# The routing's row one-hots as sixteen 16-bit comparisons with a column scalar, in a block with two mixtures of experts around attention

## The reference

```python
x = x + 0.5 * _L0_ffn_ref(_layernorm(x), router_weight, w_in, w_out, bias)
x = x + _L0_attn_ref(_layernorm(x), w_q, w_k, w_v, w_o, b_o)
x = x + 0.5 * _L0_ffn_ref(_layernorm(x), router_weight, w_in, w_out, bias)
```

## Time and profile before

| what | us |
|---|---|
| median of 3 runs (lowest, highest) | 451.69 (450.56, 455.47) |
| profiled execution, from the first to the last instruction | 448.6 |
| what lies around that span: the median less the span | 3.1 |
| TensorE busy | 401.3 (89%) |
| VectorE busy | 302.4 (67%) |
| ScalarE busy | 257.7 (57%) |
| GpSimd busy | 269.0 (60%) |
| the row one-hots (L945), four operations in all | 6.8 |
| w_lo on VectorE (L892), eight operations | 13.4 |
| TensorE's mean granted clock, as a share of full speed | 0.954 |

### The profile page before, as it was taken

How to read it: one execution, slowest core, us unless ns; L and a number is a source line. 1 busy time by engine, 2 the same in 40 slices (tenths; PEclk the granted TensorE clock), 3 DMA queues, 4 the chain that set the end, 5 groups by cost and what they waited for, 6 DMA issues and landing times.

```text
span 448.6 us, 10288 instructions
## 1 busy us (share of the span) xinstructions
PE 401.3 (89%) x2892; PEld 330.1 (74%) x2893; DVE 302.4 (67%) x605; ACT 257.7 (57%) x630; POOL 269.0 (60%) x314
## 2 busy tenths in 40 slices
PE   7305999999999989889999999988899999999995
PEld 3302788888888876758788888766478888888884
DVE  6795855685565688697767677775556576655656
ACT  2561656555655645688778788832065565565552
POOL 5846874686547817857757777410255576755760
PEclk9555899999999999999999999998899999999999
DMA  8748841111212180000000000004571112211136
GB/s 276 287 187 300 282 136 58 47 57 37 70 49 49 43 273 8 1 1 3 4 0 0 0 0 0 1 1 153 162 249 53 54 35 70 59 58 47 47 85 222
DMA packets 25736, 38.87 MB, mean 87 GB/s; under 512 B 3056, under 2 KB 20720, under 8 KB 25712
## 3 DMA queue, kind: packets, MB, share of 16 engines
q1 hardware_dynamic: 19088, 24.41, 16.1%
q0 software_dynamic: 4544, 12.07, 8.9%
q10 hardware_dynamic: 2080, 2.10, 1.4%
HBM read 29.37 MB, written 9.19 MB: 86 GB/s over the span
## 4 chain that ended last, share of the span: by engine, by line
PE 65%; DVE 16%; DMA 7%; POOL 3%; ACT 3%; issue 3%; SPq 0%; DVEq 0%; ACTq 0%; POOLq 0%
PE bank L1326 24%; PE bank L1348 12%; PE bank L1483 7%; PE bank L1494 4%; PE bank L1336 4%; DMA arena<-xn_scratch,gather_row 3%; PE bank L1450 2%; PE bank L1302 2%; PE bank L1249 2%; DMA w_out<-y_scratch 2%; PE bank L1530 2%; DVE w_lo L892 2%; POOL w_lo L511 2%; DMA y_scratch<-arena,scatter_row 1%; PE bank L1484 1%
## 5 line engine op out<-in xcount | busy, mean ns | idle before, releaser
L524 POOL DMA_INDIRECT arena<-xn_scratch,gather_row x46 | 52.8, 1149 | 58.1 <-PE bank L1302 35.6
L530 POOL DMA_INDIRECT y_scratch<-arena,scatter_row x42 | 59.3, 1412 | 31.6 <-ACT arena L701 28.6
L1326 PE MATMUL bank<-w_hi,xT_hi 128*128 x184 | 62.4, 420 | 2.1 <-ACT xT_hi L664 2.1
L1018 DVE TENSOR_TENSOR wo_lo<-w_out,wo_hi 128x1024 fp32r<-128x1024 f32 x46 | 62.0, 1348 | 2.9 <-PE bank L1348 2.0
L1023 DVE TENSOR_TENSOR gT_lo<-bank,gT_hi 128x512 fp32r<-128x512 f32 x46 | 31.7, 690 | 45.4 <-ACT gT_hi L679 45.4
L1326 PE MATMUL bank<-w_lo,xT_hi 128*128 x184 | 58.0, 396 | 0.0
L1326 PE MATMUL bank<-w_hi,xT_lo 128*128 x184 | 57.8, 395 | 0.0
L617 POOL TENSOR_TENSOR k_head<-k_hi,head_mask 128x256 fp32r<-128x256 f32 x64 | 38.8, 627 | 28.8 <-PE bank L1484 21.7
L690 ACT ACTIVATE wo_hi<-w_out 128x1024 fp32r x46 | 48.8, 1061 | 9.5 <-issue 8.7
L672 ACT ACTIVATE arena<-bank 128x512 f32<-128x512 f32 x46 | 27.5, 598 | 42.9 <-PE bank L1326 42.9
L1007 DVE TENSOR_TENSOR xT_lo<-bank,xT_hi 128x256 fp32r<-128x256 f32 x46 | 19.5, 424 | 43.0 <-ACT xT_hi L664 43.0
(11 more groups left out here) (180 smaller groups left out, 979.9 us busy)
## 6 DMA issues: line engine op xcount, KB each, us to landing
w_out<-in_win_t SPq DMA_DIRECT2D x8, 1024.0 KB, 5.1
w_out<-in_wout_t SPq DMA_DIRECT2D x16, 512.0 KB, 6.0
w_out<-y_scratch SPq DMA_DIRECT2D x16, 256.0 KB, 4.4
xn_scratch<-arena ACTq DMA_DIRECT2D x2, 1024.0 KB, 6.1
x<-in_x SPq DMA_DIRECT2D x4, 256.0 KB, 3.7
out<-x SPq DMA_DIRECT2D x4, 256.0 KB, 2.2
arena<-xn_scratch,gather_row POOLq DMA_INDIRECT x46, 3.4
y_scratch<-arena,scatter_row POOLq DMA_INDIRECT x46, 3.0
```

The costliest lines, as they stand in the source:

```text
L524: pool.indirect_dma_start(out=xb[j % 2][:, :], out_offset=None, in_=xn_dram, in_offset=bass.IndirectOffsetOnAxis(ap=gather_row[:, j:j + 1] ...
L530: pool.indirect_dma_start(out=y_dram, in_=y[j % 2][:, :], in_offset=None, out_offset=bass.IndirectOffsetOnAxis(ap=scatter_row[:, j:j + 1], ...
L1018: dve.tensor_tensor(wo_lo[:, :, :], w_out[:, bass.ds(e, 1), :, :].rearrange("p o c d -> p (o c) d"), wo_hi[u][:, :, :].bitcast(F32), ALU.s ...
L1326: last = pe.matmul(bank[2 * half + u][:, :], tok[u][:, k, :], wts[:, bass.ds(e, 1), k, half * H:(half + 1) * H], start=(part == 0 and k == ...
```

## The change

Two operations of 128 x 1024 elements, each comparing a 32-bit integer array with a 32-bit float array, become sixteen of 128 x 128, each comparing the 16-bit `col_h` with one column of the 16-bit `row_h` as a scalar per partition. The operation changes its kind from one with two array operands (tensor_tensor) to one with an array and a scalar (tensor_scalar). GpSimd makes col_h once at the start, one more constant; VectorE makes row_h from row_i in each routing. The first eight comparisons move behind the first form of block_of, the other eight behind `past`. The idle products of TensorE in the second routing go from 18 to 13.

```diff
--- before.py
+++ after.py
@@ -52,7 +52,7 @@
 LOOPED = (BLOCKS - 2 - PEELED) // 2
 AFTER = PEELED + 2 * LOOPED
 STAGES = 3
-CONSTS = 20
+CONSTS = 21
 IDENT_CONSTS = 3
 KSLOTS = 2
 P_SCALE = 2.0 ** 15
@@ -66,7 +66,7 @@
 POOL_LEAD = 1
 BIAS_STEP = 4
 
-WARM_START, WARM_RANKS, WARM_PLAN, WARM_TURNED = 12, (0, 18), (8, 6), (0, 4)
+WARM_START, WARM_RANKS, WARM_PLAN, WARM_TURNED = 12, (0, 13), (8, 6), (0, 4)
 WARM_END, WARM_CONTEXT, WARM_SCORES, WARM_LAST = 2, 4, 7, 3
 WARM_TURN = (5, 3)
 TPAIRS = TILES // 2
@@ -192,6 +192,8 @@
         before = sb("before", [P, P], F16)
         ones = sb("ones", [P, P], F16)
         col = sb("col", [P, P])
+        col_h = sb("col_h", [P, P], F16)
+        row_h = sb("row_h", [P, PAIRS], F16)
         block_edge = sb("block_edge", [P, E])
         expert_before = sb("expert_before", [P, E, E])
         block_no = sb("block_no", [P, BLOCKS])
@@ -492,6 +494,7 @@
             iota(block_no[:, :], [[1, BLOCKS]], 0, 0)
             inverse_root(0, 1)
             iota(col[:, :], [[1, P]], 0, 0)
+            then(pool.tensor_copy(col_h[:, :], col[:, :]))
             inverse_root(0, 2)
             iota(tile_edge[:, :], [[P, TILES]], 0, 0)
             inverse_root(0, 3)
@@ -940,16 +943,15 @@
                 dve.wait_ge(route_step, over_at)
                 first_at = mark(dve.tensor_reduce(first_block[:, :], over_edge[:, :, :], AX_X, ALU.add))
 
-                def one_hot_rows(q):
-                    shape = [P, q.stop - q.start, P]
-                    return mark(dve.tensor_tensor(row_hot[:, q, :], bc(row_i[:, q], 2, shape), bc(col[:, :], 1, shape),
-                                                  ALU.is_equal))
+                def one_hot_rows(some):
+                    for q in some:
+                        dve.tensor_scalar(row_hot[:, q, :], col_h[:, :], row_h[:, q:q + 1], None, ALU.is_equal)
 
 
                 dve.wait_ge(route_step, row_at)
                 if f == 0:
                     split_low(2)
-                one_hot_rows(slice(0, PAIRS // 2))
+                row_at = mark(dve.tensor_copy(row_h[:, :], row_i[:, :]))
                 dve.wait_ge(route_step, first_at)
                 placed_at = mark(dve.tensor_tensor(placed[:, :, :, :], choice[:, :, :, :],
                                                    first_block[:, :].unsqueeze(1).unsqueeze(1).to_broadcast(both), ALU.mult))
@@ -957,7 +959,8 @@
                 dve.wait_ge(route_step, placed_at)
                 block_at = mark(dve.tensor_reduce(block_of[:, :].rearrange("p (k i) -> p k i", k=TOPK), placed[:, :, :, :],
                                                   AX_X, ALU.add))
-                one_hot_rows(slice(PAIRS // 2, PAIRS))
+                dve.wait_ge(route_step, row_at)
+                one_hot_rows(range(0, PAIRS // 2))
                 if f == 0:
                     split_low(3)
                 dve.wait_ge(route_step, block_at)
@@ -966,6 +969,7 @@
                 past_at = mark(dve.tensor_tensor(past[:, :, :], bc(end_block[:, :], 1, [P, BLOCKS, E]),
                                                  bc(block_no[:, :], 2, [P, BLOCKS, E]), ALU.is_le))
                 dve.wait_ge(route_step, block_at)
+                one_hot_rows(range(PAIRS // 2, PAIRS))
                 then(dve.tensor_tensor(blk_hot[:, :, :], bc(block_of[:, :], 2, [P, PAIRS, BLOCKS]),
                                        bc(block_no[:, :], 1, [P, PAIRS, BLOCKS]), ALU.is_equal))
                 dve.tensor_tensor(blk_pair[:, :, :], blk_hot[:, :, :], bc(pair_id[:, :], 2, [P, PAIRS, BLOCKS]), ALU.mult)\
```

## The result

The changed kernel takes 455.06 us as the median of 22 runs (452.80 to 456.82). The kernel before took 452.21 beside it, in 22 runs. The ratio of the two is 1.0053, with a 95% interval of 1.0035 to 1.0071: 2.4 us slower, between 1.6 and 3.2. That lies inside the band of 1% in which the prediction called it the same, and inside its range, but it is twice the 1.2 us of its sum.

The account below looks back on a forecast made before the run. Both routings were taken to lie wholly on the path that sets the end, through VectorE. First routing +0.87 and second +0.30 us summed to +1.2, giving 452.9 us on the median, range 449.9 to 455.6.

Parts of the forecast that it names:

- Pace of a comparison, 158 ns: VectorE, both routings: a 16-bit comparison goes four columns a step and pays 65 ns for its scalar, 158 ns start to start.
- Rival 1: VectorE's comparisons: the scalar costs nothing when they stand in a row, 93 ns each; -1.0 us, 450.7; chance 0.22.
- rival 2: VectorE's comparisons stay at two or one column a step, 192 or 259 ns; +2.2 or +3.0 us; chance 0.15.
- Second routing, +0.35: VectorE: 2.26 us removed, sixteen comparisons of 2.53 and a cast of 0.08 added; blk_pair ends 0.35 us later.
- The waits on route_step: VectorE, second routing: the new waits name operations long done, so they cost nothing.
- First routing, +0.87: VectorE: GpSimd's w_lo goes in between the comparisons and block_of waits behind its second turn; blk_hot begins 0.87 us later.
- The cast on GpSimd hidden: GpSimd's cast of col, 0.29 us, lies in its 0.85 us wait for var_eps and costs nothing.
- The sum, +1.2 us: Whole kernel: +0.87 from the first routing and +0.30 from the second; 452.9 us on the median.
- The stand, 1.4 us, and the clock: TensorE, second routing: with 13 idle products it stops at about 317.0 and stands 1.4 us before the hot-row products.
- rival 3: TensorE's clock falls again just before block 0 of the second routing; 1.9 us taken, 454.8 with the sum; chance 0.13.

Follow-up runs that it names:

- e4: The changed kernel plus spare comparisons of several forms behind VectorE's second plan, results unread; 455.37 us, one run.
- e1: The changed kernel with 18 idle products in place of 13, nothing else; 453.96 us, 1.0027 of the kernel before.
- e5: The changed kernel run once more, unaltered; 455.29 us, 1.0045 of the kernel before.
- e9: The kernel before with 6 idle products in place of 18, routing untouched; 453.87 us, 1.0013 of the kernel before.
- e2: The kernel before with 13 idle products in place of 18, nothing else; 452.43 us, 0.9991 of the kernel before.
- e3: The changed kernel with two wide 32-bit comparisons at the new places, no cast or col_h, 18 idle products; 453.09 us, 1.0009 of the kernel before.
- e6: The kernel before with two wide comparisons of two packed 16-bit sources, result columns first, 13 idle products; 452.82 us, 0.9985 of the kernel before.
- e8: The kernel before with wide two-source 16-bit comparisons, 13 idle products and VectorE's w_lo(3) and w_lo(4) moved later; 451.31 us, 0.9964 of the kernel before.
- e10: The changed kernel with its sixteen narrow comparisons at the old operations' places, 18 idle products; 453.16 us, 1.0018 of the kernel before.

## Why the prediction was right, and where it was off

The forecast was 452.9 us, from 449.9 to 455.6, within 1% with 0.91. The range and the class held. In its own terms, of +1.2 us, the change came to +2.4.

- **Pace of a comparison, 158 ns.** Measured 162.5. The scalar's price is measured, 60 ns in each instruction (65 predicted); four columns a step fits the spacings of e4, though the width wasn't varied. Rival 1 (93 ns) and rival 2 (192 or 259) are out; e4 gives 100 ns for the form without a scalar.
- **Second routing, +0.35.** Measured +0.46. The cast took 0.12 us from start to start, where I had 0.08 from the chain's piece for rank_i, and the pace's 4 ns make 0.07 over sixteen. The waits on route_step added none, as said.
- **First routing, +0.87.** Measured +0.65. The order of events was right in each step: five comparisons, GpSimd's turn, the rest, w_lo(3), GpSimd's second turn with block_of behind it. Most of the 0.22 is a step of counting. I let three whole comparisons follow GpSimd's end; the sixth had been issued before and ends with the turn, so two were left, and w_lo(3) began 5.21 us behind w_lo(2)'s start, where my figures have 29.27 - 23.87 = 5.40.
- **The cast on GpSimd hidden.** Right: 0.49 us of waiting for var_eps was left of it.
- **The sum, +1.2 us.** This holds for everything but the idle products: e1 has 1.0027, +1.2 us. In part that is luck: the first routing was put 0.22 us too high and the second 0.11 to 0.16 too low.
- **The stand, 1.4 us, and the clock.** This is the step that failed: the sum puts the five products fewer at nothing. I wrote that TensorE stands 1.4 us, counting the five products that go at 0.22 us each off a place in time, and put the low clock aside as rival 3 with 0.13. How long 13 products last depends on the clock they meet: 2.97 us in one profile, 4.65 in the other, so the stand was 3.17 and 1.49 (1.65 in e4). In both the clock then was at 1.2 GHz before block 0; in e4 it wasn't. Block 0 took 5.05 and 6.00 us, +1.15 and +2.1. Over all runs the ratios of the changed kernel lie 0.8 to 1.2 us above that of e1, and 14 of 35 runs show a low mean clock against 1 of 12. Rival 3 had the place, and a price of 1.9 us that lies between the two. That the 0.8 to 1.2 us are the clock at block 0 is argued from these profiles and counts, since no run without a profile shows where its clock was low.
- **What stays open.** What decides whether the clock is low at block 0. The three profiles in which it was low differ: it fell at the end of the stand (the changed kernel, first profile), it fell behind the plan (e5), or it had been low since the idle products (e9). e2, with 13 products and a stand of 1.03 us, and e4, with 1.65, don't have it, and each kernel has a profile or two. The first mixture's block 0 also ran longer at the low clock in the changed kernel (until 51 us, before until 47). From its first turning to the next it took 6.66 and 6.61 us there, 5.77 before and 6.04 in e1. e3 has the same with two wide operations and 18 products, until 50.7 and 6.64 us, and so has e9 (6.59), so I don't put it down to the change; it isn't settled, and at 0.6 to 0.9 us it would matter.

Where did the gain of the 16-bit form go? It was there: 128 columns cost 0.033 us in place of 0.134, which saves 0.80 us of 1024. But these were one operation with a fixed part of 0.06, and became eight with 0.13 each (0.1625 - 0.033, fixed part and scalar together): 1.04 in place of 0.06. The difference, 0.98 - 0.80, is the 0.17 to 0.18 that eight comparisons take more than the wide one (1.30 against 1.13).

## What to carry to other kernels

An operation that is split to reach a faster mode pays its fixed part, and that of a column scalar, in each piece: here 0.13 us a piece, as much as 128 columns had cost at the slow rate. By these numbers, an estimate, a piece would have to be wider than 0.13 / (0.001046 x 3/4) = 166 columns to gain. A wide operation with two packed 16-bit inputs (e6) beats both forms, if the engine that reads the result doesn't pay for the layout.

A count of idle products is a length of time only at a known clock. Where the wait that they cover gets longer, taking some away is a risk: too many cost what the last one reaches over, and with too few a block of work ran at half the clock in some executions here.

Where two engines wait each other out, ask for each long operation which small one stands behind it: one subtraction moved behind the plan took 1.14 us off it, while the rewriting of the comparisons made the plan longer (0.65) or, in the form of e6, left it as it was (0.02).

## What the runs showed of the hardware that I had not expected

- With the columns of the stationary operand 16 bytes apart, 16 small products of TensorE took 1.15 us in place of 0.57 (e6, e8), and their loads 1.06 in place of 0.47. The Trainium skill, "Advanced Engine Details and Errata", section "Memory Cachelines", speaks of 16-byte lines in SBUF and of a penalty when each access falls in another line; the trace agrees, without showing the cause.
- GpSimd got its turn in the middle of eight narrow comparisons, at 26.87 us, and in e10 in both groups. It had two turns ahead of gather_row in the kernel before too; what differs is its own wait. Its subtraction took 2.38 us among narrow comparisons, and 2.56 in e3, where it asked while a wide one ran.
- The 32-bit block_of as scalar of a 16-bit comparison costs as much as the 16-bit row_h (shortest records 249 and 251 ns in e4, 0.74 us for four of either). So the cast to row_h, 0.07 us from start to start in the first routing and 0.12 in the second, may be saved where the scalar is fp32; with the int32 row_i itself it wasn't tried.
- In all 12 profiles, of kernels that differ only around the routing, the clock at the end of the first gather was at either level, and came back to 2.4 GHz between 46 and 51 us. Block 0 of the first mixture took 5.74 us (e2) to 6.66 with it. This scatter alone is as large as the effects sought here, and only distances between places in one profile told them apart.
